# Dense experts' first product in half-precision parts, with the weights split beforehand during the third attention

## The reference, cut to what matters

```python
x = x + tanh(g_xattn[2]) * attention(ctx, ctx, layernorm(x))      # third attention, 16 heads, 375 keys
x = x + tanh(g_ffn[2]) * dense(layernorm(x), w1, b1, w2, b2)      # dense experts
x = x + tanh(g_xattn[3]) * attention_one_head(layernorm(x), ctx)
x = x + tanh(g_ffn[3]) * fp4_ffn(layernorm(x))

def dense(x, w1, b1, w2, b2):      # w1 [8, 256, 1024], w2 [8, 1024, 256]
    tokens = x.reshape(8, 224, 256)                # expert e has batches 2e and 2e + 1
    h = gelu(einsum('etd,edf->etf', tokens, w1) + b1[:, None, :])
    return (einsum('etf,efd->etd', h, w2) + b2[:, None, :]).reshape(x.shape)
```

## Time and profile before

| | |
|---|---|
| three runs | 1383.01, 1387.66, 1391.0 us; median 1387.66 |
| the profiled execution | 1383.34 us, span 1381.6 us, mean granted clock of PE 0.997 |
| busy in the span | PE 96%, DVE 80%, ACT 50%, GpSimd 30% |
| third attention | about 791 to 1043 us, one body 14.7 to 15.1 us |
| dense experts | about 1043.7 to 1158.7 us, one expert 13.9 us of PE |

### The profile page before, as it was taken

The page is one execution under the profiler, slowest core; times in us unless marked ns, Lnnn a source line. Parts: engine busy times, 40 slices in busy tenths (PEclk is TensorE's granted clock), DMA queues, the critical chain, the costliest instruction groups (busy, mean ns, idle before and its releaser), DMA issues. The chain is left out here.

```text
span 1381.6 us, 37331 instructions
## 1 busy us (share of the span) xinstructions
PE 1323.2 (96%) x12290; PEld 1013.7 (73%) x12290; DVE 1106.8 (80%) x3711; ACT 686.2 (50%) x1639; POOL 412.5 (30%) x580
## 2 busy tenths in 40 slices
PE   7899999999999999999999999999999999998998
PEld 5678888755667777776655578888888888986666
DVE  7798887688889998888778877677664886678997
ACT  2666767544345555555434356666663223442222
POOL 2333246444543344447134432332330000000000
PEclk9999999999999999999999999999999999999999
DMA  5634455231333333334111243333346451660000
GB/s 167 166 114 127 129 154 159 85 116 50 85 102 101 95 89 86 90 88 120 32 57 47 70 117 98 101 94 94 102 135 185 149 175 47 159 146 15 16 15 23
DMA packets 134461, 138.16 MB, mean 100 GB/s; under 512 B 38986, under 2 KB 121677, under 8 KB 134221
## 3 DMA queue, kind: packets, MB, share of 16 engines
q1 hardware_dynamic: 134332, 136.51, 34.8%
HBM read 100.98 MB, written 35.48 MB: 99 GB/s over the span
## 5 line engine op out<-in xcount | busy, mean ns | idle before, releaser
L1156 DVE TENSOR_REDUCE negm<-ps 112x1 f32<-112x375 f32 x512 | 260.3, 542 | 102.1 <-PE ps L1280 100.3
L1280 PE MATMUL ps<-kst,qst 96*112 96x375 f16 x768 | 240.3, 335 | 10.7 <-DVE negm L1156 5.6
L866 ACT ACTIVATE p<-ps 125x448 f32<-125x448 f32 x336 | 175.1, 545 | 84.6 <-PE ps L1308 71.5
L835 POOL TENSOR_TENSOR qst<-m_row,diag 16x448 f16<-16x448 f16 x128 | 128.3, 1030 | 274.4 <-ACT m_row L945 269.6
L1295 PE MATMUL ps<-qst,kst 112*125 112x224 f16 (+1 forms) x1152 | 206.5, 261 | 2.9 <-ACT p L866 1.7
L1295 PEld LDWEIGHTS ps<-qst,kst 112*125 112x125 f16 (+1 forms) x1152 | 149.5, 137 | 29.7 <-ACT p L866 3.6
L1809 PE MATMUL ps<-fw,xs_e 128*128 128x512 f16 x672 | 158.9, 379 | 0.0
L1140 DVE TENSOR_SCALAR ps<-ps 125x448 f32<-125x448 f32 x192 | 120.0, 629 | 29.0 <-PE ps L1295 28.9
L1152 DVE CUSTOM_DVE_ANT_0 with_mask<-ps,mask_add 112x375 f16<-112x375 f32 x256 | 134.2, 545 | 9.7 <-issue 8.2
L1280 PEld LDWEIGHTS ps<-kst,qst 96*112 96x112 f16 x768 | 96.0, 129 | 44.6 <-DVE negm L1156 14.4
L1203 PE MATMUL ps<-wkv_split,ctxT 128*125 128x256 f16 x864 | 118.5, 273 | 0.0
(11 more groups left out here) (264 smaller groups left out, 2615.7 us busy)
## 6 DMA issues: line engine op xcount, KB each, us to landing
k_split<-ks SPq DMA_DIRECT2D x48, 375.0 KB, 3.6
kst<-k_split SPq DMA_DIRECT2D x96, 187.5 KB, 2.9
fw<-in_w SPq DMA_DIRECT2D x16, 1024.0 KB, 7.3
qst<-q_split SPq DMA_DIRECT2D x96, 112.0 KB, 2.4
kst<-k_split SPq DMA_DIRECT2D x96, 93.8 KB, 2.7
stage<-in_ctxT SPq DMA_DIRECT2D x16, 375.0 KB, 4.0
rows<-x SPq DMA_DIRECT2D x48, 112.9 KB, 2.2
q_split<-qs SPq DMA_DIRECT2D x96, 56.0 KB, 2.7
```

The lines of the kernel that those rows point to most:

```text
L835: pool.tensor_tensor(m_stack[q][m_rows, 4 * hg:4 * hg + 4, :], g.m_row[q][m_rows, :].rearrange("p (o s) -> p o s", o=1) .to_broadcast([n_m ...
L866: act.activation(p[p_of[hg]][kt], ps[0:KR, BK_ST + n % 2, 0:4 * S], ACT.Exp).then_inc(s_exp, 1)
L1156: dve.tensor_reduce(g.negm[1 - par][:, h:h + 1], scored, AX_X, ALU.max, negate=True).then_inc(s_max, 1)
L1280: mm = pe.matmul(ps[0:S, BK_S + h % 2, 0:SK], g.q_stack[q][0:96, h, :], g.k_stack[q][0:96, h // 2, :], start=True, stop=True)
```

## The change

The first product h is computed from half-precision parts: w1 = high + low, rows = high + low, and three products (high x high, high x low, low x high) accumulate in f32. The parts of the rows are made in the dense stage (ACT the high one, DVE the low one). The parts of w1 are made in the third attention: SyncE loads w1 of an expert into `fw[0]`, GpSimd splits it in four pieces of 512 columns into `fw[1]` (bodies 0 to 4 and 11 to 13), SyncE stores the parts (1 MB) to DRAM one body later and loads w1 of the expert after the next. The dense loads then read parts instead of w1, the same number of bytes, and the first of them wait for the last store. PE's turning of rows and its first product now wait for the low part. Core of the diff:

```diff
+SPLIT_AT = {0: 0, 1: 1, 2: 2, 3: 3, 4: 4, 11: 5, 12: 6, 13: 7}
+STORED_AT = {1: 0, 2: 1, 3: 2, 4: 3, 11: 4, 12: 5, 13: 6, 14: 7}
@@ attention, SyncE, after load_stack(1 - par, 1) @@
-                if layer == 2 and isinstance(i, int) and i == B - 2:
+                opening = not first and isinstance(i, int) and i == -1
+                if layer == 2 and opening:
+                    for e in range(2):
+                        load_first_weights(sp, a, g, e, s_raw1)
+                if layer == 2 and isinstance(i, int) and i in STORED_AT:
+                    e = STORED_AT[i]
+                    held(sp, g, s_parts, e + 1)
+                    sp.dma_start(g.dram_w1[e], dense_parts(g, e % 2)).then_inc(s_stored[e % 2], 16)
+                    if e + 2 < E:
+                        load_first_weights(sp, a, g, e + 2, s_raw1)
+                if layer == 2 and isinstance(i, int) and i == B - 1:
+                    for e in range(2):
+                        held(sp, g, s_stored[e], 16 * E // 2)
                     load_dense(sp, a, g, 0, 0, g.s_w1)
-                if layer == 2 and isinstance(i, int) and i == B - 1:
                     load_dense(sp, a, g, 0, 1, g.s_w2)
                     load_dense(sp, a, g, 1, 0, g.s_w1)
@@ attention, GpSimd @@
+            def split_first_weights(e):
+                whole = g.fw[0][:, e % 2 * 2048:(e % 2 + 1) * 2048]
+                high, low = (dense_parts(g, e % 2)[:, n * 2048:(n + 1) * 2048] for n in range(2))
+                pool.wait_ge(s_raw1[e % 2], 16 * (e // 2 + 1))
+                if e > 1:
+                    pool.wait_ge(s_stored[e % 2], 16 * (e // 2))
+                for n in range(4):
+                    cols = slice(n * 512, (n + 1) * 512)
+                    carry(pool, g, 1)
+                    step(pool.tensor_copy(high[:, cols], whole[:, cols]))
+                    step.sync()
+                    low_part = pool.tensor_tensor(low[:, cols], whole[:, cols], high[:, cols], ALU.subtract)
+                    if n < 3:
+                        step(low_part)
+                low_part.then_inc(s_parts, 1)
+                pool.wait_ge(s_parts, e + 1)
@@ attention, GpSimd body, between the query split and the m_row multiplications @@
+                if layer == 2 and isinstance(i, int) and i in SPLIT_AT:
+                    split_first_weights(SPLIT_AT[i])
@@ load_dense @@
-        sp.dma_start(g.fw[0][:, par * n:(par + 1) * n].rearrange("p (c f) -> p c f", c=KC),
-                     a["w1"][index].rearrange("(c p) f -> p c f", p=128)).then_inc(sem[par], 16)
+        sp.dma_start(g.fw[0][:, par * n:(par + 1) * n].bitcast(F16), g.dram_w1[index]).then_inc(sem[par], 16)
@@ experts_dense, ScalarE @@
-                        act.activation(xnT[q][:, :, :], ps[:, 0, 0:KC * W].rearrange("p (c s) -> p c s", c=KC),
-                                       ACT.Copy).then_inc(s_xnT, 1)
+                        act.activation(xs[q][:, 0, :, :], turned, ACT.Copy).then_inc(s_xhi, 1)
@@ experts_dense, VectorE, between the norming and gate_up_weights @@
+                    if there(i + 1, E):
+                        dve.wait_ge(s_xhi, i + 2)
+                        dve.tensor_tensor(xs[1 - turn.u][:, 1, :, :], turned, xs[1 - turn.u][:, 0, :, :],
+                                          ALU.subtract).then_inc(s_xlo, 1)
@@ experts_dense, TensorE @@
-                        at_least(pe, s_xnT, i + 1)
+                        at_least(pe, s_xlo, i + 1)
-                        pe.wait_ge(s_xnT, i + 2)
+                        pe.wait_ge(s_xlo, i + 2)
+                            k = 0
                             for c in range(KC):
-                                mm = pe.matmul(ps[:, 1 + f % HB, 0:W], w1[q][:, c, f * 128:(f + 1) * 128],
-                                               xnT[q][:, c, :], start=(c == 0), stop=(c == KC - 1))
+                                for l, r in ((0, 0), (0, 1), (1, 0)):
+                                    mm = pe.matmul(ps[:, 1 + f % HB, 0:W], w1[q][:, l, c, f * 128:(f + 1) * 128],
+                                                   xs[q][:, r, c, :], start=(k == 0), stop=(k == 3 * KC - 1))
+                                    k += 1
```

More of the change, by code:

```diff
@@ L157, in build @@
                     for i in range(2)]
+        g.dram_w1 = nc.dram_tensor("w1_parts", (E, 128, 2 * KC * F), F16, kind="Internal").ap()
         g.s_aw = [sem(f"attention_weights{i}") for i in range(3)]
@@ L527, in attention @@
     s_bo_rows = sem("bias_rows")
+    if layer == 2:
+        s_raw1 = [sem(f"w1_raw{i}") for i in range(2)]
+        s_parts = sem("w1_parts")
+        s_stored = [sem(f"w1_stored{i}") for i in range(2)]
     s_ctx = [sem(f"ctx_loaded{i}") for i in range(2)]
@@ L680, in body @@
                     load_gates(sp, a, g, layer)
-                if layer == 2 and isinstance(i, int) and i == B - 2:
+                opening = not first and isinstance(i, int) and i == -1
[11 more added lines that the diff above has]
+                        held(sp, g, s_stored[e], 16 * E // 2)
                     load_dense(sp, a, g, 0, 0, g.s_w1)
-                if layer == 2 and isinstance(i, int) and i == B - 1:
                     load_dense(sp, a, g, 0, 1, g.s_w2)
                     load_dense(sp, a, g, 1, 0, g.s_w1)
-                opening = not first and isinstance(i, int) and i == -1
                 if opening:
@@ L1886, in _, with dense_parts, load_first_weights @@
                 keep_clock(pe, g, 3, WAITS["end of tiles"])
+def dense_parts(g, p):
+    return g.fw[1][:, p * 2048:(p + 1) * 2048].bitcast(F16)
+def load_first_weights(sp, a, g, e, sem):
+    sp.dma_start(g.fw[0][:, e % 2 * 2048:(e % 2 + 1) * 2048].rearrange("p (c f) -> p c f", c=KC),
+                 a["w1"][e].rearrange("(c p) f -> p c f", p=128)).then_inc(sem[e % 2], 16)
 def load_dense(sp, a, g, e, which, sem):
@@ L1909, in experts_dense @@
     s_w1, s_w2 = g.s_w1, g.s_w2
-    s_xn, s_t, s_xnT, s_h, s_gelu, s_y, s_x = (sem(n) for n in ("xn", "transposed", "xnT", "h", "gelu", "y", "x"))
+    s_xn, s_t, s_h, s_gelu, s_y, s_x = (sem(n) for n in ("xn", "transposed", "h", "gelu", "y", "x"))
     s_rows, s_dve, s_m = sem("rows_counted"), sem("dve"), sem("wq_wk")
+    s_xhi, s_xlo = sem("xnT_high"), sem("xnT_low")
     gate = g.gates[0:S, 6:7]
@@ L1921, in experts_dense @@
         b2 = sb("b2", [S, E, D])
-        xnT = [sb(f"xnT{i}", [128, KC, W]) for i in range(2)]
+        xs = [sb(f"xs{i}", [128, 2, KC, W], F16) for i in range(2)]
+        turned = ps[:, 0, 0:KC * W].rearrange("p (c s) -> p c s", c=KC)
         hT = [sb(f"hT{i}", [128, FT, W]) for i in range(2)]
         acc = [sb(f"acc{i}", [S, D]) for i in range(2)]
-        w1 = [g.fw[0][:, p * 2048:(p + 1) * 2048].rearrange("p (c f) -> p c f", c=KC) for p in range(2)]
+        w1 = [g.fw[0][:, p * 2048:(p + 1) * 2048].bitcast(F16).rearrange("p (l c f) -> p l c f", l=2, c=KC)
+              for p in range(2)]
         w2 = [g.fw[1][:, p * 2048:(p + 1) * 2048].rearrange("p (f d) -> p f d", f=FT) for p in range(2)]
```

## The result

The changed kernel takes 1401.75 us (median of 7 runs, 1395.79 to 1403.57); the kernel before took 1384.38 beside it (7 runs, 1383.01 to 1391.0). The ratio is 1.0107, 95% interval 1.0089 to 1.0124: some 15 us slower, and above the range that was forecast. The profiled execution of the changed kernel has a span of 1399.8 us, 18.2 more than before.

The account below looks back on a forecast made before the run. PE was taken as the bound, with DVE near full and bounding the changed dense stage. Terms -0.1 + 1.0 + 0 + 0 + 1.2 = +2.1 us gave 1389.8 us against the 1387.66 median, range 1382 to 1399.

Parts of the forecast that it names:

- The transfers in the bodies: Third attention: 2 MB on SyncE's queue delay stacks 0.8 to 1.4 us, within slack 2.0; 0, bounds 0 and 1 a body.
- Rival C: Third attention: megabytes slower than 376 GB/s, keys and queries late, six bodies each lose the excess; 1397.5 us, chance 0.13.
- The opening: Third attention's start: both raw loads ahead of keys make PE wait 1.1 to 1.3 us for a stack; +1.2.
- GpSimd: Third attention: splits of 7.8 us fit GpSimd's 8.64 us idle window before m_row; cost 0.
- rival B: Third attention: GpSimd's splits overrun because their pieces are slower; chance 0.10.
- The dense stage: DVE becomes the bound, PE's 12 us saving turns into waits; -0.1 us, bounds -0.7 and +0.5.
- the term of the low part: Dense stage: DVE's added subtraction of 448 columns from PSUM, 0.65 us an expert, bounds 0.55 and 0.75.
- y(1): Dense stage, second product of expert 1: waits for DVE's first update and starts at 1066.67 as before.
- The stage after: One-head stage behind the dense stage: PE idles before it and starts at half clock; +1.0 us.
- D: Dense stage: rounded weights arrive before 1061.09, DVE's 7.96 us of idling vanish; 1378 us, chance 0.04.
- E: Dense stage: half-precision products paced by weight loads of 0.13 us, PE's cycle 14 us again; 1389 us, chance 0.06.

Follow-up runs that it names:

- e2: Kernel before with only the raw w1 loads and the 1 MB stores, no split, dense stage as before; third attention 14.8 us longer.
- e1: Kernel before with only the eight GpSimd splits, no raw loads or stores; third attention 5.4 us longer, time 3.6 us up.
- e4: Changed kernel with every split and store one free body later, first raw loads still in the opening; body 0 lost 4.5 us for 6.9.
- e5: e4 with the first two experts' raw loads moved from the opening to bodies 0 and 1; body 0 lost 0.0, bodies 5 and 14 lost 11.8 us.
- e12: e1 with each split in eight pieces of 128x256 for four of 128x512; body 0's loss fell from 4.1 to 1.4 us.
- e3: Changed kernel with one split instead of eight, all experts reading the first one's w1; no change in the time, dense stage -1.2 us.
- e10: Changed kernel with splits and transfers placed where runs found room, earlier weight roundings and PE fillers around the dense stage; ratio 0.9991 to the kernel before.

## Why the prediction was wrong

**The transfers in the bodies**, "0, bounds 0 and 1 us a body", is the step that failed: 10.4 us alone (e2), 5.2 in the changed kernel (bodies 4 and 5, the 0.8 of bodies 2 and 3 being GpSimd's as in e1). I counted the megabytes once, against the slack of one body, and found the stack "0.8 to 1.4 us later"; in bodies 2 to 4 it came 7.5 to 9.3 us behind the keys' store for 4.9 to 5.6, so 1.9 to 4.1 later. This has three faults: the 2 MB, priced at 5.6 us, took 8.5 to 10.3 us in bodies 1 to 4 from their first issue to their last landing, the keys up to 8.7 us (3.4 before), while the engines, at full share, moved 313 GB/s and not 376 (row below); a late stack also delays the next megabytes, which then stand nearer to the next keys; and a loop that is longer than PE's body (16.6 for 14.7) loses its excess anew in each.

```profile
880.50:888.50 8.00, 7.97 (x82) 6.79 (x80) 7.17 (x16) 6.32 (x16) 6.36 (x13) 1.00 0.96 313
```

Rival C had the place and the sign, and six bodies at a fixed excess; the waits came in bodies 4 and 5 (0.4 and 2.9 us), with a half-clock spell behind the second (0.55 from 898.0 to 901.4), and 12 and 13 lost 0.0 and 0.5.

**The clock in the attention** stands in no term: the sum prices half clock behind the dense stage alone. Two spells behind PE's waits cost 3.4 of the 14.2 us.

**The opening**, "+1.2, bounds 0 and 4": PE waited 2.7 us, and in e2 and e4, where nothing else falls into body 0, a half-clock spell makes it 4.4 (e2, and e4 against e5). The direction and place were right; the stack was released 5.1 us later where I had 2.7.

**GpSimd**, "0": the length was right (7.7 us for 7.8, 8.1 in body 0), and so was the lack of an overrun. The step that failed is the one from "there the subtraction never left 2125 to 2138 ns" to a price of 0. Those rows show how long GpSimd takes, and the price fell on VectorE, whose durations I didn't compare: 5.4 us alone (e1), 1.7 of them half clock. VectorE's operations between SBUF and SBUF lost up to 0.86 us each: casts of 1x256 and `tensor_scalar` of 112x8, which read one tensor, and `tensor_tensor` of 112x8, which reads two (0.85 us for 0.15); GpSimd's own grew from 1.16 to 1.22. So the two engines do hold each other up, rival B's ground, but on the other engine than the one I watched, and not only in instructions that read two tensors. The cast took 1.13 us for 0.27 and ended with GpSimd's operation (821.28 and 821.14), and 0.64 with half the piece (e12).

**The dense stage**, -0.1 forecast, -0.9 measured (-1.2 in e3): the mechanism was right, the term of the low part (0.65) too large. It is 0.62 us long but overlaps its neighbour, 0.54 from start to start; six of them less the 4.00 us of waits that vanished give -0.8. That PE would wait for the low part before each product was wrong: it did so once, 3.12 us. Nor did y(1) wait for VectorE.

**The stage after**, +1.0 forecast, +1.2 measured. The +1.0 was my estimate of what half clock at its start costs, and no run shows that price; the changed kernel's trace shows a granted clock of 0.50 to 0.54 from 1171 to 1181, and PE busy for 4.52 us of it. Over the nine kernels with half-precision products it takes 223.4 us on average, over the five others 222.1. That the half clock at its start is the cause was only argued, and it is not the whole of it: e10 has no spell there and took 223.6, e2 has full-precision products and took 223.8. The cause of the rest stays open.

Rivals D and E are out: the wait for the weights to be rounded shrank only as the low parts moved into it, and the products took 0.096 us each (48 between 1154.70 and 1159.30); their weight loads took 0.098 us in the median, where E had 0.13.

## What to carry to other kernels

Before putting bulk transfers into a loop whose data go through DRAM, add up the loop from one dependent load to the next (the compute that it releases, the store that this compute feeds, every landing in between, with the bulk beside it) and compare it with the body's length. One short transfer behind 2 MB took 5 us longer, and moving 1 MB of it to the other side of the stack gave 10 us back with the same bytes. Look at the granted clock behind every new wait of PE: here waits of 2.5 to 3.5 us were mostly followed by 3.4 or 6.8 us at half clock, which costs another 1.7 or 3.4. Work given to an idle GpSimd must be checked against what VectorE does between SBUF and SBUF in the same microseconds (up to 0.86 us more an operation here), and cut so that both the longest piece and the whole fit. A saving on one of two nearly full engines is worth little until the other one's chain starts earlier or gets shorter: 12 us on PE gave 0.9.

## What was not expected of the hardware

- A second queue gave no protection: stores of keys landed in 8.2 us (median) beside 2 MB issued by ScalarE at the same moment, and in 6.3 us when stored 2.6 to 4.9 us behind 1 or 2 MB on their own queue; alone they need 3.4.
- An operation of VectorE on 1x256 elements took four times as long (1.13 for 0.27 us), while GpSimd was inside one of 128x512, and 0.64 beside one of 128x256; operations of VectorE that read PSUM kept their 0.53 us beside it.
- Two losses of this pipeline were not additive: 4.1 and 4.4 us in the same body gave 6.9, since each alone brought a half-clock spell of 1.7 us and both together brought one. Taking one away (e5) moved 4 us of loss to body 14, where two spells came behind a wait of 3.5 us.
